# ScalarE scales the contexts, the RMS gain moves behind the depooling product, and a one-row product carries the input bias

## What is computed

```python
h = rmsnorm(layernorm(x), g_res)                     # 512 x 256 per sequence
h = einsum('bld,ed->ble', h, W_in) + b_in            # input product and bias
h_patch = rmsnorm(ctx, g_init)[..., :256]            # ctx: 1601 x 512; the norm is over all 512
u = c * h_patch; s[t] = a * s[t-1] + u[t]            # decaying sum over the rows ("depool")
x = x + (s[plug] + h)                                # plug: a row index per token, from the lengths
x = x + moe(layernorm(x))                            # 8 experts, top 2, F = 1024
```

## Time and profile before

| | us |
|---|---|
| median of 3 runs | 485.46 (485.13 to 485.64) |
| profiled execution | 485.91 |
| its span on the core | 484.2 |
| up to the experts' first product | 109.3 |
| the experts' steps and the end | 374.9 |

### The profile page before, as it was taken

One profiled execution on the slowest core, in us unless ns is written; L12 is line 12 of the kernel. 1 busy time (PEld: TensorE's weight loads), 2 busy tenths in 40 slices (PEclk: granted clock), 3 DMA queues, 4 the chain that ended last, 5 costly groups with the idle time before them and its releaser, 6 DMA issues.

```text
span 484.2 us, 10484 instructions
## 1 busy us (share of the span) xinstructions
PE 422.1 (87%) x2557; PEld 366.8 (76%) x2558; DVE 259.7 (54%) x750; ACT 192.6 (40%) x334; POOL 155.0 (32%) x130
## 2 busy tenths in 40 slices
PE   0768984329899999999999999999999999999980
PEld 0557864327688988888888888888988888888870
DVE  7977857988753355334553553365355334552230
ACT  3446444203442445324544443454445324542220
POOL 5354440022042234223432432253234223432321
PEclk9979886558999999999999999999999999999996
DMA  6856787400719112811136128112711211211121
GB/s 194 308 175 218 261 265 220 167 24 22 271 26 292 32 22 27 287 32 22 25 102 220 22 42 283 22 22 70 254 22 22 32 32 22 27 30 30 22 32 11
DMA packets 33077, 50.92 MB, mean 105 GB/s; under 512 B 3335, under 2 KB 25095, under 8 KB 33063
## 3 DMA queue, kind: packets, MB, share of 16 engines
q1 hardware_dynamic: 24983, 38.44, 23.6%
q0 software_dynamic: 8080, 12.33, 13.1%
HBM read 39.36 MB, written 11.40 MB: 105 GB/s over the span
## 4 chain that ended last, share of the span: by engine, by line
PE 73%; DVE 6%; issue 2%; DMA 2%; POOL 1%; DVEq 1%; ACT 0%; POOLq 0%; ACTq 0%
PE bank L1329 63%; PE bank L1352 6%; PE bank L1336 2%; DMA dg<-depool_rows,plugi 1%; DVE ctx_sb L904 1%; PE bank L1262 1%; DMA out<-yblk,itok 1%; PE bank L1283 1%; POOL dg L443 1%; DVE split L1124 0%; DVE split L323 0%; DVE batch L992 0%; PE bank L1208 0%; POOL out L482 0%; DVE onehot_lo L988 0%
## 5 line engine op out<-in xcount | busy, mean ns | idle before, releaser
L1329 PE MATMUL bank<-split,xT_hi 128*128 x592 | 166.8, 404 | 1.4 <-DVE xT_lo L1089 1.4
L1098 DVE TENSOR_TENSOR hmul<-gact,bank 128x512 f32<-128x512 f32 x74 | 50.9, 688 | 145.4 <-ACT gact L611 145.4
L482 POOL DMA_INDIRECT out<-yblk,itok x37 | 78.3, 2115 | 150.3 <-ACT yblk L618 138.3
L1329 PEld LDWEIGHTS bank<-split,xT_hi 128*128 128x128 f32 x592 | 106.9, 190 | 22.4 <-issue 2.2
L1329 PE MATMUL bank<-split,hT 128*128 (+1 forms) x888 | 115.7, 287 | 1.5 <-issue 0.8
L1329 PEld LDWEIGHTS bank<-split,hT 128*128 128x128 f32 x888 | 108.8, 192 | 2.1 <-issue 1.3
L611 ACT ACTIVATE gact<-bank 128x512 f32<-128x512 f32 x74 | 44.2, 597 | 158.1 <-PE bank L1329 158.1
L1329 PE MATMUL bank<-split,xT_lo 128*128 x296 | 93.2, 396 | 0.0
L474 POOL DMA_INDIRECT xblk<-z_rows,gidx x40 | 40.7, 1018 | 106.3 <-DVE gidx L1111 100.4
L323 DVE TENSOR_TENSOR split<-raw,split (+1 forms) x22 | 50.4, 2292 | 37.1 <-ACT split L317 35.9
L1329 PEld LDWEIGHTS bank<-split,xT_lo 128*128 128x128 f32 x296 | 56.0, 189 | 13.3
(11 more groups left out here) (184 smaller groups left out, 312.9 us busy)
## 6 DMA issues: line engine op xcount, KB each, us to landing
raw<-in_L_ffn_w SPq DMA_DIRECT2D x24, 1024.0 KB, 8.2
ctx_sb<-in_ctx SPq DMA_DIRECT2D x4, 1024.0 KB, 6.4
x_all<-in_x SPq DMA_DIRECT2D x4, 512.0 KB, 8.2
depool_rows<-gact SPq DMA_DIRECT2D x4, 512.0 KB, 3.0
out<-x_all SPq DMA_DIRECT2D x4, 512.0 KB, 4.6
z_rows<-z SPq DMA_DIRECT2D x4, 512.0 KB, 3.8
xblk<-z_rows,gidx POOLq DMA_INDIRECT x40, 2.8
out<-yblk,itok POOLq DMA_INDIRECT x37, 4.7
```

The lines of the kernel that those rows point to most:

```text
L482: pool.indirect_dma_start(out[:, :], bass.IndirectOffsetOnAxis(ap=itok[:, q:q + 1], axis=0), yblk[:, q, :], None, compute_op=ALU.add).then ...
L1098: dve.tensor_tensor(hmul[:, cols], gact[:, cols], p_lin[part][:, :], ALU.mult)\
L1329: mm = pe.matmul(out_, xp, w_, start=start and n == 0, stop=stop and n == 2)
```

## The change

Three edits that belong together, in what the diff names `scaled_ctx`, `depooled` and `through_win`:

1. The context rows are multiplied by their row factor `rs` on ACT (a Copy with a scale per partition), ahead of `hn` in ACT's order, and no more by `rs * ginit` on DVE.
2. The column factor `ginit` is multiplied in where the depooled rows leave PSUM; the decaying sum goes along the rows, so a column factor commutes with it.
3. The bias, which was added there, is now added to the PE result of `through_win`: after the two products of every tile comes a third with a stationary row of ones (1 partition x 128) and the bias as one row (1 partition x 256).

```diff
-        bin_ = sb("bin", [P, D], f32)
+        bin_ = sb("bin", [1, D], f32)
+        ones_row = sb("ones_row", [1, P], f32)
...
-            sp.dma_start(bin_[:, :], b_in.unsqueeze(0).broadcast_to([P, D])).then_inc(s["small_in"], 16)
+            sp.dma_start(bin_[:, :], b_in.unsqueeze(0)).then_inc(s["small_in"], 16)
...
+            def scaled_ctx(b):
+                act.wait_ge(s["rs_ready"], b + 1)
+                if b >= 1:
+                    act.wait_ge(s["depmm_ready"], TPB * b)
+                for j in range(TPB):
+                    act.activation(hp[:, j, :], ctx_sb[:, b % 2, j, 0:D], ACT.Copy, scale=rs[:, b % 2, j:j + 1])\
+                       .then_inc(s["hp_ready"], 1)
...
                 if k < B:
+                    scaled_ctx(k)
                     norm_first(k)
...
+            dve.memset(ones_row[:, :], 1.0).then_inc(s["consts"], 1)
...
-            dve.wait_ge(s["consts"], 2)
+            dve.wait_ge(s["consts"], 3)
...
-                dve.wait_ge(ctx_in[b], 16)
+
+            def depooled(b):
                 if b == 0:
                     dve.wait_ge(s["small_in"], 16 * 5)
-                if b >= 1:
-                    dve.wait_ge(s["depmm_ready"], TPB * b)
-                for j in range(TPB):
-                    dve.scalar_tensor_tensor(hp[:, j, :], ctx_sb[:, b % 2, j, 0:D], rs[:, b % 2, j:j + 1],
-                                             ginit[:, :], ALU.mult, ALU.mult).then_inc(s["hp_ready"], 1)
...
-                                      bin_[:, :].unsqueeze(1).broadcast_to([P, 2, D]), ALU.add)\
+                                      ginit[:, :].unsqueeze(1).broadcast_to([P, 2, D]), ALU.mult)\
...
-                pe.wait_ge(s["consts"], 2)
+                pe.wait_ge(s["consts"], 3)
...
-                        mm = pe.matmul(pH[j // 2][:, (j % 2) * D:(j % 2 + 1) * D],
+                        pe.matmul(pH[j // 2][:, (j % 2) * D:(j % 2 + 1) * D],
                                        hnT[b % 2][:, j, k * P:(k + 1) * P], win[:, k, :],
-                                       start=(k == 0), stop=(k == KD - 1))
+                                       start=(k == 0), stop=False)
+                    mm = pe.matmul(pH[j // 2][:, (j % 2) * D:(j % 2 + 1) * D], ones_row[:, :], bin_[:, :],
+                                   start=False, stop=True)
                     mm.then_inc(s["hmm_ready"], 1)
```

More of the change, by code:

```diff
@@ L790, in norm_first @@
                                          ALU.mult, ALU.mult).then_inc(s["nb1_ready"], 1)
-                dve.wait_ge(ctx_in[b], 16)
+            def depooled(b):
                 if b == 0:
                     dve.wait_ge(s["small_in"], 16 * 5)
-                if b >= 1:
-                    dve.wait_ge(s["depmm_ready"], TPB * b)
-                for j in range(TPB):
-                    dve.scalar_tensor_tensor(hp[:, j, :], ctx_sb[:, b % 2, j, 0:D], rs[:, b % 2, j:j + 1],
-                                             ginit[:, :], ALU.mult, ALU.mult).then_inc(s["hp_ready"], 1)
-            def depooled(b):
                 if b >= 1:
```

## The result

The changed kernel takes 488.93 us (median of 8 runs, 486.39 to 490.38), the kernel before 485.47 beside it. The ratio is 1.0077 with a 95% interval of 1.0055 to 1.0099: it is slower by 0.77%, where I had forecast 0.4% faster. The gain that I had worked out for ScalarE and VectorE came (0.43% in the run without the products), and the one-row product, dear as in rival D, took nearly three times as much away. Part of that is its price at full clock, and more of it a spell at half clock in the last sequence.

What follows compares the result with a forecast made beforehand. The gather-to-gather loop was taken to bound the head, with PE late after the change: x complete at 73.25 for 75.41, 2.15 us, less 0.15 for the clock, 2.0 off 485.91 gives 483.9, median 483.4; range 481.6 to 485.3.

Steps and rivals of the forecast that it cites:

- rival D: In through_win: one-row products cost 0.87 us each in place of 0.45, kernel 4.5 us slower, 490.0; chance 0.08.
- What bounds the kernel: First 110 us: a loop from gather to gather, hanging on gather(1)'s start, sets when the experts' part begins.
- Part 1: Row-factor products from DVE to ACT: four Copies 1.7 us, gather(1) at 37.0, the gather loop gains 2.45 us.
- the likeliest case: The forecast itself, with first(1) on PE not at full clock: 482.6 to 484.5 us, chance 0.55.
- Part 2: In depooled on DVE: multiplying by ginit in place of adding the bias costs 0.
- Part 3: Four one-row products in each through_win, 0.45 us each taken: 1.8 us for each sequence, 7.2 in all.
- The path: PE, full from first(1) to through_win(3), completes x at 73.25, a little behind the gather loop's 72.95.
- Behind x(3): The routing tail (logits(2), places, the table) waits for x(3) and moves along with it.
- Rival C: Half clock hits through_win(3) or the experts' start: gain only 0.2 to 1.3 us, time 484.2 to 485.3; chance 0.22.
- The range: Whole kernel: time forecast between 481.6 and 485.3 us.

Runs made afterwards that it cites:

- e3: The changed kernel with the bias product on 128 rows (stationary of 1/128, bias on all 128 partitions): 482.19 us, ratio 0.9948 to the kernel before.
- e4: The changed kernel with the bias put first, as one one-row product of 512 columns per bank: 481.20 us, ratio 0.9941 to the kernel before.

## Why the prediction was wrong

*What bounds the kernel:* right. The time moved with the completion of x(3) in every run, by the table above.

*Part 1:* right, nearly to the tenth. The four Copies on ACT take 1.71 us (forecast 1.7; one is 0.493), vin(1) is written at 21.36 (21.4), bmask at 25.94 (25.65), first(1) starts at 26.33 (26.0), gather(1) at 36.94 (37.0). The clock of first(1) was 0.52, as I had assumed for the likeliest case.

*Part 2:* 0, right. The multiplication takes 1.29 us for two, against 1.28 for the addition in the earlier trace rows.

*Part 3:* here it failed, at the value taken, which was the low one of two ends. I took 0.45 us for a one-row product and wrote that "the passes stream the same columns"; measured are 0.82 at full clock (1.69 less the 0.87 that a tile takes without it, 3.46 us for four tiles), near the high end of 0.87. Two passes of the same columns on 128 rows do take 0.43 (e3). The term that I put at nothing is the turn of shape, 0.40. I had it in rival D as the price of two weight loads that stand open, and dismissed it because the loads hide "in every product of the trace"; but all products of that row have one shape, 128*128, and no product of the kernel before works on fewer than 128 rows. What stands open is also not quite what rival D had: the first load after each turn, one of the small shape and one of the full, while the second one-row load follows beside (two in 0.29 us). Rival D's own sum was x(3) complete at 79.95 and 490.0 us: the profiled execution had it at 79.48 and 490.32. I gave it 0.08.

*The rule of the page "TensorE: Matmul & The Clock Gate" of the Trainium skill, Part 3, "The mechanism":* that a load overlaps a running product only when the row groups differ. The runs show something else: equal shapes overlap (0.43 us for a 128-row product, e3, and one-row loads under one-row products, e4), and it is the change of shape that stands open (0.33 us of idle load engine). The same section of the Trainium skill also lets a load go ahead when it targets the background weight buffer, which my prediction left out; that would cover the loads of equal shape, but no run here shows the buffer. The statement of the same page of the Trainium skill, section on LDWEIGHTS, that a load's time follows its columns and not its rows agrees: 0.184 us for one row, 0.190 for 128.

*The path:* I had PE as the later of two chains by 0.3 us, so there was next to nothing to hide a mis-sized product. Forecast for x(3) was 73.25, measured 79.48, 6.2 later, and 16 x 0.40 = 6.4 us of turns. That the two agree so well is partly luck. Through_win(3) was 3.9 us longer than forecast (7.2, measured 11.1), of which the turns at full clock explain 1.3 (6.7 for 5.4) and the clock 2.6 (4.4 in place of 1.8). And it started only 2.3 us later than forecast (67.60 for 65.3), though three stages with turns had cost 4.4 by then: PE was 2.1 us faster between, 1.4 of it in first(3), which ran at full clock in 3.1 us and had taken 4.5.

*Behind x(3):* right. The experts' first product starts at 113.33, where it started at 109.28: 4.05 us later, like x(3), which is 4.07 later.

*Rival C* was right in kind: the half clock did fall on through_win(3). I priced it at 1.8 us for products of 0.45; with turns the whole stage lost 4.4 to it (11.1 less the 6.7 of the execution with 32 rows).

*The range* left out rival D knowingly. An unknown price with ends of 0.45 and 0.87 that is multiplied by 16, on a path without slack, moves the time by 6.7 us; a chance of 0.08 for the upper half of it was not worked out from any row.

## What to carry to other kernels

An operation whose shape no row of the trace shows has no price there, and "the same columns" is only a part of it: before it goes 16 times onto a path without slack, take its dear end as seriously as its cheap one. Here the turns of a small product between full ones could be taken away by padding its rows with a stationary of 1/128, and made fewer by gathering several products into one: the same change with 128 rows is 0.5% faster than the kernel before (0.9945 and 0.9948 in two measurements), and with one row 0.7 to 0.8% slower. And a single execution of a kernel whose clock spells move says little about a difference of 1%: the same program with 64 rows took 482.92 us once, and 488.74 as the median of four executions on another chip, while the kernel before took 485.3 on both.

## What the runs showed of the hardware

- A product on 1, 32 or 64 rows between products on 128 rows costs 0.40 us more than one on 96 or 128 rows at full clock (1.69 against 1.29 to 1.30 us per tile), at two passes each. At half clock the turns cost about 0.59 (3.15 us per tile, against 6 passes of 0.427 = 2.56; in first(1) of the same trace two passes take 0.85 or 0.86).
- The load engine stands idle for 0.33 us at each turn at full clock, and then loads one row in 0.184 us, 128 rows in 0.190. Between products of one shape, full or one-row, the loads run beside the products.
- A Copy with a scale per row from SBUF takes 0.493 us at 128x256 on ACT, 0.02 more than the one from PSUM in the earlier trace rows; four in a row 1.71.
- The same program can meet through_win(3) at full or at half clock (64 rows: 6.7 us in one execution, 10.9 in another, on another chip); what decides that was not settled.
